# Weights on a second DMA queue, and seven row transfers in place of thirteen, in a four-layer equivariant convolution kernel

## The reference

```python
x = x + conv(_gn(x), L0_conv_weights, L0_conv_bias)
...
x = x + conv(_gn(x), L3_conv_weights, L3_conv_bias)
# conv: for each of the 15 partitions of (i0, i1, o0, o1):
#   Y += einsum(X, weights[i]) over the axes that the partition ties or sums, / denom
#   and Y + sum(bias)
```

## Time and profile before

| what | value |
|---|---|
| median of 3 runs | 1950.24 us |
| lowest, highest | 1950.18, 1955.7 us |
| the profiled execution: span | 1947.9 us |
| median less the span | 2.3 us |
| PE busy, DVE busy | 1573.7 us, 1297.6 us |
| ACT busy, POOL busy | 81.8 us, 295.6 us |
| moved by DMA | 821.81 MB, mean 422 GB/s |

### The profile page before, as it was taken

One profiled execution on the slowest core, in us unless ns is written; L12 is line 12 of the kernel. 1 busy time (PEld: TensorE's weight loads), 2 busy tenths in 40 slices (PEclk: granted clock), 3 DMA queues, 4 the chain that ended last, 5 costly groups with the idle time before them and its releaser, 6 DMA issues.

```text
span 1947.9 us, 42202 instructions
## 1 busy us (share of the span) xinstructions
PE 1573.7 (81%) x19274; PEld 965.8 (50%) x19278; DVE 1297.6 (67%) x1260; ACT 81.8 (4%) x85; POOL 295.6 (15%) x670
## 2 busy tenths in 40 slices
PE   6888888888888899997777777777787787777785
PEld 5877888887888853443333333333333333333332
DVE  5988889888988846775555555555555555555554
ACT  0111110011111110000000000000000000000000
POOL 7433444333333310000000000000000000000000
PEclk9999999999999998999999999999999999999998
DMA  9999999999999979999999999999999999999998
GB/s 379 415 413 415 425 428 429 429 427 429 429 427 430 427 316 384 429 429 430 432 431 431 430 431 431 430 430 432 431 430 431 431 432 431 430 431 431 431 430 370
DMA packets 58796, 821.81 MB, mean 422 GB/s; under 512 B 8376, under 2 KB 8504, under 8 KB 9080
## 3 DMA queue, kind: packets, MB, share of 16 engines
q1 hardware_dynamic: 39048, 551.77, 66.8%
q10 hardware_dynamic: 19696, 269.40, 32.4%
HBM read 551.75 MB, written 269.09 MB: 421 GB/s over the span
## 4 chain that ended last, share of the span: by engine, by line
DMA 74%; PE 15%; DVE 6%; issue 4%; SPq 0%; ACT 0%; DVEq 0%
DMA early<-strip_in 28%; DMA early<-pairs 25%; DMA out<-early 21%; PE ps L881 11%; DVE ring_own L618 3%; PE ps L758 2%; DVE early L728 1%; DVE early L736 1%; PE ps L783 0%; PE ps L889 0%; PE ps L888 0%; PE ps L862 0%; PE ps L809 0%; PE ps L769 0%; ACT early L583 0%
## 5 line engine op out<-in xcount | busy, mean ns | idle before, releaser
L881 PE MATMUL ps<-ring_own,mixer 128*128 128x512 f32 x1252 | 593.0, 631 | 140.7 <-DMA ring_own<-strip_in 114.1
L758 PE MATMUL ps<-early 128*64 128x66 f32 x16896 | 554.9, 225 | 123.8 <-DMA early<-pairs 112.0
L618 DVE TENSOR_REDUCE ring_own<-early 128x32 f32<-128x2048 f32 x264 | 590.6, 2281 | 79.6 <-DMA early<-pairs 79.5
L758 PEld LDWEIGHTS ps<-early 128*64 128x64 f32 x16896 | 537.4, 139 | 141.1 <-DMA early<-pairs 96.0
L728 DVE SCALAR_TENSOR_TENSOR ring_own<-ps,row_sum,stage 128x512 f32<-128x512 f32 (+3 forms) x233 | 301.6, 1295 | 322.0 <-PE ps L881 322.0
L881 PEld LDWEIGHTS ps<-ring_own,mixer 128*128 128x128 f32 x1252 | 246.8, 202 | 487.2 <-issue 471.9
L881 PE MATMUL ps<-early,mixer 128*128 128x512 f32 x800 | 376.5, 627 | 89.6 <-DMA early<-strip_in 81.6
L728 DVE SCALAR_TENSOR_TENSOR early<-ps,row_sum,stage 128x1024 f32<-128x1024 f32 (+2 forms) x152 | 192.5, 1267 | 199.1 <-PE ps L881 199.1
L881 PEld LDWEIGHTS ps<-early,mixer 128*128 128x128 f32 x800 | 157.0, 201 | 308.7 <-issue 294.9
L443 POOL TENSOR_TENSOR gram_all<-gram_all,stage 128x512 f32<-128x512 f32 x132 | 167.6, 1291 | 0.0
L736 DVE SCALAR_TENSOR_TENSOR ring_own<-ps,row_sum,stage 128x488 f32<-128x488 f32 (+43 forms) x308 | 133.4, 475 | 0.0
(11 more groups left out here) (137 smaller groups left out, 101.9 us busy)
## 6 DMA issues: line engine op xcount, KB each, us to landing
early<-pairs SPq DMA_DIRECT2D x132, 2080.0 KB, 15.3
ring_own<-strip_in SPq DMA_DIRECT2D x78, 2048.0 KB, 49.1
out<-ring_own ACTq DMA_DIRECT2D x78, 2048.0 KB, 38.5
early<-strip_in SPq DMA_DIRECT2D x50, 2048.0 KB, 49.0
out<-early ACTq DMA_DIRECT2D x50, 2048.0 KB, 38.5
const<-const_f SPq DMA_DIRECT2D x1, 773.5 KB, 23.7
ring_own<-dia_pair SPq DMA_DIRECT2D x1, 640.0 KB, 23.5
ring_own<-half_in SPq DMA_DIRECT2D x1, 512.0 KB, 34.5
```

What stands on the lines that cost most here:

```text
L618: nc.vector.tensor_reduce(part_sum[:, t % sums], pairs_of(s), AX.XYZ, ALU.add).then_inc(summed, 1)
L758: last = mm(regions(parity)[lane:lane + WIDE, m // BANK_REGIONS, m % BANK_REGIONS], chunk(slot, k, False), chunk(slot, k, True), start=ope ...
L881: last = mm(ps[:, first + at // BANK, 0:piece], mixer[:, :, :].rearrange("p a m -> p (a m)"), buf[:, at:at + piece], start=True, stop=True)
```

## The change

Two edits. The four loads of weights and four of biases go from the front of SP's queue to the front of ACT's, so that the tiles' DMAs are the first that SP issues. And the two place buffers are interleaved by row block, as are `step_m` and `step_mean` in one tile `step_both`, so that one transfer of 3072 bytes from each of 16 partitions brings a row block of both: 6 transfers at quads 5 to 10 and `brow` at quad 11, in place of 12 at quads 5 to 16 and `brow` at quad 17.

```diff
-        step_m = sb("step_m", [97, LAYERS, ROWS])
-        step_mean = sb("step_mean", [97, LAYERS, ROWS])
+        step_both = sb("step_both", [97, 2, LAYERS, ROWS])
+        step_m, step_mean = step_both[:, 0], step_both[:, 1]
...
-        place = [place_buf[:, m * wsize:(m + 1) * wsize].rearrange("p (l r o) -> p l r o", l=LAYERS, r=6)
-                 for m in range(2)]
+        place_rows = place_buf[:, 0:2 * wsize].rearrange("p (r m l o) -> p r m l o", r=6, m=2, l=LAYERS)
+        place = [place_rows[:, :, m].rearrange("p r l o -> p l r o") for m in range(2)]
...
-            for layer in range(LAYERS):
-                sp.dma_start(wt[:, layer], weights[layer].rearrange("k c o -> c k o")).then_inc(weights_in, 16)
-                sp.dma_start(bias_sb[:, layer], biases[layer].rearrange("(z k) -> z k", z=1)).then_inc(weights_in, 16)
             for t in range(0, len(tiles), 2):
...
-            sp.wait_ge(matrices_in, 16 * 13)
+            sp.wait_ge(matrices_in, 16 * 7)
...
         def _(act):
+            for layer in range(LAYERS):
+                act.dma_start(wt[:, layer], weights[layer].rearrange("k c o -> c k o")).then_inc(weights_in, 16)
+                act.dma_start(bias_sb[:, layer], biases[layer].rearrange("(z k) -> z k", z=1)).then_inc(weights_in, 16)
             for q in range(len(spans)):
...
-                if 5 <= q < 17:
-                    m, rb = divmod(q - 5, 6)
-                    dst = (step_m, step_mean)[m]
-                    act.dma_start(dst[rb * CH:(rb + 1) * CH], place[m][:, :, rb, :]).then_inc(matrices_in, 16)
-                if q == 17:
+                if 5 <= q < 11:
+                    rb = q - 5
+                    act.dma_start(step_both[rb * CH:(rb + 1) * CH], place_rows[:, rb]).then_inc(matrices_in, 16)
+                if q == 11:
                     act.wait_ge(beta_done, 1)
                     act.dma_start(step_mean[96:97], brow[:, :, :]).then_inc(matrices_in, 16)
```

More of the change, by code:

```diff
@@ L434, in add_quad @@
                     pool.wait_ge(rows_added, len(spans))
-                    pool.wait_ge(matrices_in, 16 * 13)
+                    pool.wait_ge(matrices_in, 16 * 7)
                     nc.gpsimd.tensor_tensor(spread[:, late], row_sum[:, late].unsqueeze(2).to_broadcast([BLK, per_block, SUB]),
@@ L558, in _ @@
                     act.wait_ge(place_done, 1)
-                if 5 <= q < 17:
-                    m, rb = divmod(q - 5, 6)
-                    dst = (step_m, step_mean)[m]
-                    act.dma_start(dst[rb * CH:(rb + 1) * CH], place[m][:, :, rb, :]).then_inc(matrices_in, 16)
-                if q == 17:
+                if 5 <= q < 11:
+                    rb = q - 5
+                    act.dma_start(step_both[rb * CH:(rb + 1) * CH], place_rows[:, rb]).then_inc(matrices_in, 16)
+                if q == 11:
                     act.wait_ge(beta_done, 1)
                     act.dma_start(step_mean[96:97], brow[:, :, :]).then_inc(matrices_in, 16)
-                if q == max(len(spans) - 2, 17):
-                    act.wait_ge(matrices_in, 16 * 13)
+                if q == max(len(spans) - 2, 11):
+                    act.wait_ge(matrices_in, 16 * 7)
                     act.wait_ge(rows_added, len(spans) - late_quads)
@@ L643, in _ @@
                     link(tt(dia_cov[:, :], dia_cov[:, :], c("blocks"), ALU.mult))
-            dve.wait_ge(matrices_in, 16 * 13)
+            dve.wait_ge(matrices_in, 16 * 7)
             dve.wait_ge(sum_added, len(tiles))
```

## The result

Over eleven runs each the changed kernel has a median of 1957.23 us (1954.94 to 1961.93) beside 1951.95 us (1948.59 to 1956.37) for the kernel before. The ratio is 1.0026, 95% interval 1.0014 to 1.0037: 5.1 us slower by the ratio and 5.3 by the medians, inside the 0.3% that I had called no change, though the interval is clear of 1, and about 1.5 us more than the +3.65 forecast. The forecast time was 1953.9 us; of the 3.3 us above it, 1.7 are the kernel before itself, whose median was 1950.24 us when I predicted. The profiled execution has a span of 1954.0 us, 6.1 above that of before. At the end of the first pass, where DVE reduces the features, it is 5.57 us late (690.31 against 684.74 us in the two chains of waits), so nearly all of the difference arises in the first pass.

What follows compares the result with a forecast made beforehand. The DMA engines' byte stream bounds the kernel. Start -2.9, weights' own packets +0.65, slowing +2.0, hole +7.4, placing -3.5 sum to +3.65 us on 1950.24: 1953.9 us, range 1945 to 1959.

Steps and rivals of the forecast that it cites:

- The start: SP's first tile DMAs: issued at 0.75 us, 2.93 us earlier, with tile bytes from 1.6 us; -2.9 us.
- The weights' own packets and the slowing: Weights beside tiles on the DMA engines: 0.65 us of their own plus 2.0 us for slowed neighbours.
- the price by bytes: Slowing of tiles by 60 weight packets an engine if cost follows bytes (60 KB against 24): 0.8 us.
- the price by packets: Slowing of tiles by 60 weight packets an engine at 0.075 us per packet: 4.7 us.
- The second rival: Small packets slow the tiles: weights cost 4.7 us, placing saves only 2.1, +7.85 us in all, 1958.1 us; chance 0.20.
- When the weights land: ACT's queue: weight packets take turns with SP's packets, so they land at 34.1 us; before, POOL had them at 5.04.
- The chain: Late weights delay POOL (quad 0 added at 70.3), ACT's quad 2 copy (71.3), PE's quad 4 and SP's issue (76.6 us).
- The hole: DMA engines stand still from 70.1 to 77.5 us, with tiles 24 and 25 issued late; +7.4 us.
- The placing: Placing transfers of the matrices: twelve at 0.41 us become six at 0.25 us; -3.5 us, between -4.3 and -2.1.
- The bias row: Model for the new placing transfers, one packet an engine like them: its turn's DMA took 0.13 us more.
- the ring: Waits from POOL through ACT's copy of quad 2 and PE's quad 4 to SP's tile issue at 76.6 us (before: 66.6).

Runs made afterwards that it cites:

- the packed weights: Changed kernel with the weights laid out by the host as 16 rows of 3840 bytes and the biases as one row: ratio 0.9983 to the kernel before.
- the extra transfer: Changed kernel with one more weights transfer (240 packets, 15 KB) ahead of the others on ACT's queue: ratio 1.0069 to the kernel before.
- the queue alone: Kernel before with only the weights and biases moved to ACT's queue, its thirteen placing transfers kept: ratio 1.0033 to the kernel before.
- the seven transfers alone: Changed kernel with the eight weight and bias loads back at the head of SP's queue: ratio 1.0003 to the kernel before.
- the late matrices: Changed kernel with POOL building the matrices in pieces behind the quads it adds, and ACT placing them at quads 14 to 20: ratio 0.9987 to the kernel before.
- both cures together: Changed kernel with weights as one row a partition and matrices built late in pieces: ratio 0.9972 to the kernel before, median 1947.95 us.
- the split: Changed kernel with two layers' weights and biases on ACT's queue and two ahead of the tiles on SP's: ratio 0.9972 to the kernel before.

## Why the prediction was right

**The start, -2.9 us.** Right. Tile bytes flow in the half microsecond from 1.5 us, where the kernel before had them in that from 4.5. ACT's table load went behind the weights (4.62 us); ACT's next work was at 19.80, so it cost nothing.

**The weights' own packets and the slowing, +2.65 us.** Too high. In the 35 us after its first tile byte the changed kernel's SP queue moved 13.94 MB and that of before 14.48, 0.54 MB or 1.3 us less. Less the 0.65 of their own, the slowing was about 0.6 us for 60 packets an engine, near the price by bytes (0.8) and far from the price by packets. The second rival's 4.7 us did not occur.

**When the weights land, 34.1 us.** Measured 33.54. With the measured slowing of 0.6 us in place of 2.0 the same sum gives 32.7, so part of the close agreement is luck. The counts of the queues confirm the turns packet by packet, and the landing of the joined transfers agrees; the packed weights (7.88 for 4 to 6 us) and the extra transfer (6.9 for 9.9 us) agree in direction, not in size. The Trainium skill's rule of some 9 to 17 descriptors before a switch ("DMA: Bandwidth & Descriptors", Queues, rings and completion order) does not describe these transfers, whose counts are equal even within a microsecond. The prediction had also applied that rule to one queue only: by it the tiles' queue, too, would send several rows at its turn, so "beside one tile row" and a landing before 10 us did not follow from it.

**The chain.** POOL took 29.2 us for the matrices (predicted 30.5), had quad 0 added at 68.3 (70.3), PE started quad 4 at 69.62 (71.3), and its first pair of tiles took 5.7 us (5.3 predicted from the earlier trace rows): after 11.84 us of idling the clock was granted at 0.50, its 1.2 GHz level, from 69 to 73 us and at 1.00 from there. The issue came at 75.29 (76.6). The 1.3 us on POOL belong to the late start and not to the new layout: with the old layout and late weights the matrices took 29.3 us (the queue alone), with the new layout and early weights 30.5 (the seven transfers alone). Why is not shown.

**The hole, +7.4 us.** Measured 9.6. This is the term that was mis-sized most. Its far end came 1.3 us early, its near end more so: the stream was dry at about 68 and not 70.1. That makes some 8.2 us. The other 1.4 were lost after the stream had started again (333 GB/s from 77 to 79 us, 362 from 81 to 85), while SP issued one DMA every 3.95 us (79.24, 83.20, 87.15). The prediction had put this at nothing, with the stream back at its full rate at once; what held it below 428 GB/s there is not shown. As for the near end, I had carried over what the kernel before loses between 40 and 70 us, and 2.0 us of slowing; of the former the changed kernel lost little (423 GB/s from 40 to 50 us and 425 to 60, where 413 had stood), so it ran into its dry spell sooner.

**The placing, -3.5 us.** Measured -2.1: 4.3 us before; after, the stretches from 90 to 150 us lose 2.2 us:

```profile
90.00:100.00 10.00, 9.64 (x312) 9.49 (x310) 8.54 (x5) 1.06 (x1) 3.54 (x12) 1.00 1.01 406
100.00:120.00 20.00, 16.06 (x499) 15.52 (x494) 17.25 (x8) 2.10 (x2) 7.23 (x16) 1.00 1.00 410
120.00:140.00 20.00, 16.15 (x501) 15.75 (x503) 17.16 (x8) 2.10 (x2) 8.51 (x21) 1.00 1.01 419
140.00:150.00 10.00, 7.98 (x251) 7.70 (x248) 8.48 (x5) 1.05 (x1) 4.17 (x10) 1.00 1.00 411
```

The bias row was a poor model: it is alike in packets, one an engine, but carries 1.5 KB and not 48. The measured saving is the bound of -2.1 that the second rival had, and that rival's price for the placing was thus the right one.

Together -2.9 + 1.3 + 9.6 - 2.1 = +5.9 us, beside 5.57 at the end of the first pass; the difference is of the size of what the kernel before loses around 40 to 60 us and the new one does not. The direction and the case were right: late weights, POOL at the head of the ring, and a hole. The errors of the weights' slowing (-1.4) went against those of the hole (+2.2) and the placing (+1.4).

## What to carry to other kernels

Count a small load by its packets, not by its bytes, and against what the other queue holds at that moment: 62 packets an engine beside tile rows and the constants took 32 us here, 2 to 4 packets were there before 8 us, and the same small packets, half on each queue beside each other, before 4. A load that is moved out of the way of the stream must be looked at from its reader: who is in order behind the engine that waits for it, and how many buffers later does that reach the engine that feeds the stream. Taking the waiting work out of the head of that engine's program (the late matrices) or cutting the packets are both cures, and so is splitting the load over the two queues. The best came out 0.28% below the kernel before: both cures together, and the split.

## What the runs showed of the hardware

While both had packets waiting, two queues of one set of DMA engines took turns one for one: 584 to 584 and 109 to 109 packets in the run with one more transfer, 419 to 420 in the changed kernel from 5 to 20 us, whatever their sizes of 64 and 16640 bytes. From 20 to 30 us the changed kernel has 584 to 558; that some engines had by then sent all their weights is likely and not shown.

A copy from SBUF to SBUF from 16 partitions cost the stream more than its bytes: 288 KB took 2.2 us of it, where 288 KB of tiles take 0.7 at 428 GB/s, the same in six transfers as in twelve. In rows of 384 bytes the same 288 KB took 4.3 us.

In the run with one more transfer, ACT's ninth issue in a row took 5.05 us where the others took 0.32 to 0.56:

```profile
3.95 0.36 ACTq L548 DMA_DIRECT2D ring_own<-weights  x1
4.34 5.05 ACTq L549 DMA_DIRECT2D bias_sb<-bias  x1
```

It is the run that put the most packets on ACT's queue, and with eight issues in a row none took over 0.67 us. A full queue that holds up the engine that issues would fit, but no run varies this alone. ACT had nothing else to do there, so this run does not show what such an issue costs either.
